# The turned maxima of an attention block: four 32 by 32 block transposes on VectorE in place of a TensorE transpose and a ScalarE copy

## What is computed

```python
h = _layernorm(x) * (1 + ca) + sa
qkv = h @ qkv_w.T                                  # q, k, v of 16 heads
scores = einsum('bhqd,bhkd->bhqk', q, k) * scale
out = einsum('bhqk,bhkd->bhqd', softmax(scores), v)
x = x + ga * (out.reshape(B, S, D) @ proj_w.T + proj_b)
h = _layernorm(x) * (1 + cb) + sb
x = x + gb * ffn(h)        # ffn: a base layer, and the adapter whose encoder loses least
```

## Time and profile before

| what | value |
|---|---|
| median of 3 runs | 971.41 us (971.34 to 973.51) |
| the profiled execution, its own time | 969.45 us |
| its span in the trace | 967.6 us |
| busy: TensorE, VectorE, ScalarE, GpSimd | 933.6, 791.9, 656.6, 373.1 us |

### The profile page before, as it was taken

One profiled execution on the slowest core, in us unless ns is written; L12 is line 12 of the kernel. 1 busy time (PEld: TensorE's weight loads), 2 busy tenths in 40 slices (PEclk: granted clock), 3 DMA queues, 4 the chain that ended last, 5 costly groups with the idle time before them and its releaser, 6 DMA issues.

```text
span 967.6 us, 16714 instructions
## 1 busy us (share of the span) xinstructions
PE 933.6 (96%) x5890; PEld 487.8 (50%) x5890; DVE 791.9 (82%) x1629; ACT 656.6 (68%) x1295; POOL 373.1 (39%) x497
## 2 busy tenths in 40 slices
PE   6899999999999999999999999999999999999998
PEld 5443444444445555555454555555445455644486
DVE  4799989999888888877897987876887778888365
ACT  2148788888688677666779677675777766657930
POOL 4050265226456454121756545121655321115320
PEclk9889999999999999999999999999999999999999
DMA  6933052253454211555150511536133500141001
GB/s 179 144 73 45 23 111 63 57 116 87 77 83 74 58 42 36 73 92 162 46 94 13 94 57 36 83 65 167 46 67 51 78 12 25 46 128 55 30 6 50
DMA packets 51427, 68.78 MB, mean 71 GB/s; under 512 B 12347, under 2 KB 35648, under 8 KB 51332
## 3 DMA queue, kind: packets, MB, share of 16 engines
q1 hardware_dynamic: 50108, 66.84, 32.1%
q0 software_dynamic: 384, 0.79, 0.6%
q10 hardware_dynamic: 852, 0.09, 0.1%
HBM read 29.31 MB, written 12.59 MB: 43 GB/s over the span
## 4 chain that ended last, share of the span: by engine, by line
PE 75%; DVE 11%; ACT 5%; DMA 4%; SPq 3%; issue 2%; POOL 1%; ACTq 0%; DVEq 0%
PE pE L851 25%; PE pM L851 21%; PE pO L851 20%; DVE mx L1350 7%; PE pX L851 7%; DMA QO<-lo 2%; ACT P L1176 2%; SPq L1955 1%; DMA xin<-in_x 1%; DVE junk L1544 1%; ACT h2l_full L1263 1%; SPq L2015 1%; DMA P<-in_wmod 0%; ACT h1l_full L1217 0%; DVE junk L1487 0%
## 5 line engine op out<-in xcount | busy, mean ns | idle before, releaser
L1350 DVE TENSOR_REDUCE mx<-pM 128x1 f32<-128x512 f32 x458 | 298.9, 683 | 41.6 <-PE pM L851 39.4
L1176 ACT ACTIVATE P<-pM 128x512 f32<-128x512 f32 x464 | 260.2, 603 | 71.5 <-PE pM L851 70.1
L1350 DVE TENSOR_REDUCE mx<-pE 128x1 f32<-128x512 f32 x428 | 284.5, 682 | 29.4 <-PE pE L851 28.4
L1176 ACT ACTIVATE P<-pE 128x512 f32<-128x512 f32 x413 | 240.6, 603 | 81.0 <-PE pE L851 79.9
L851 PE MATMUL pO<-P,V 128*17 128x512 f32 x2048 | 260.6, 604 | 0.3 <-ACT P L1176 0.2
L851 PE MATMUL pM<-KO,QO 48*128 48x512 f32 x458 | 181.7, 451 | 7.7 <-DMA QO<-lo 6.0
L851 PE MATMUL pE<-KO,QO 48*128 48x512 f32 x428 | 178.4, 444 | 1.4 <-DVE mx L1350 0.6
L851 PE MATMUL pM<-QO,KO 50*128 50x512 f32 x464 | 173.6, 433 | 0.9 <-DVE mx L1350 0.4
L851 PE MATMUL pE<-QO,KO 50*128 50x512 f32 x413 | 169.8, 438 | 1.3 <-DVE mx L1350 0.7
L851 PEld LDWEIGHTS pM<-QO,KO 50*128 50x128 f32 x464 | 80.2, 187 | 85.3 <-issue 59.6
L851 PEld LDWEIGHTS pE<-QO,KO 50*128 50x128 f32 x413 | 73.5, 186 | 96.9 <-issue 76.4
(11 more groups left out here) (362 smaller groups left out, 1392.5 us busy)
## 6 DMA issues: line engine op xcount, KB each, us to landing
outs<-osb SPq DMA_DIRECT2D x31, 256.0 KB, 2.0
KO<-hi SPq DMA_DIRECT2D x56, 128.0 KB, 4.0
QO<-hi SPq DMA_DIRECT2D x56, 128.0 KB, 5.6
x<-in_x SPq DMA_DIRECT2D x20, 256.0 KB, 3.5
out<-x SPq DMA_DIRECT2D x16, 256.0 KB, 2.1
AT<-outs SPq DMA_DIRECT2D x15, 256.0 KB
asum<-wsum SPq DMA_DIRECT2D x15, 256.0 KB
KO<-lo SPq DMA_DIRECT2D x28, 128.0 KB, 4.0
```

What stands on the lines that cost most here:

```text
L1176: e.activation(P[:, u % 3, j, :], bank(s), ACT.Exp).then_inc(*empties(s))
L1350: e.tensor_reduce(mx[:, hq % 2, k:k + 1, kh], bank(s), AX.X, ALU.max, negate=True).then_inc(*empties(s))
```

## The change

The `mturn` step leaves TensorE and ScalarE. VectorE does it with four transposes of 32 by 32 blocks, from `mhl` in SBUF to `mT` in SBUF, and raises a semaphore of its own, `s_mT`, for which the DMA queues wait. The step no longer takes a PSUM bank, and the planner holds it at the front of the queue "quiet" instead of "short". The lag of 1.2 units, `LEAD` and the other constants stay.

```diff
-BANKED = {"modmm", "modT", "modT2", "ln1turn", "qk", "v", "mturn", "oturn", ...
+BANKED = {"modmm", "modT", "modT2", "ln1turn", "qk", "v", "oturn", ...
-SHORT = {"ln1turn", "mturn", "oturn", "atturn", "xturn", "select", "modT2"}
+SHORT = {"ln1turn", "oturn", "atturn", "xturn", "select", "modT2"}
+QUIET = {"mturn", "oput", ...
...
-                waiting["short"].insert(0, ("mturn", m // 32 - 1))
+                waiting["quiet"].insert(0, ("mturn", m // 32 - 1))
...
# tensor
-                elif kind == "mturn":
-                    pe.wait_ge(s_mhl, s[1] + 1)
-                    e.transpose(o[0:32, 0:128], mhl[:, s[1] % 2, :], ident).then_inc(*fills(s))
...
# scalar
-                    act.wait_ge(*full(*s))
-                    e.activation(mT[0:32, hq % 2, :], bank(s)[0:32, 0:128], ACT.Copy).then_inc(*empties(s))
-                    if hq == 0:
-                        act.wait_ge(*emptied(*s))
+                elif s == ("mturn", 0):
+                    act.wait_ge(s_mT, 1)
...
# vector
+                elif kind == "mturn":
+                    hq = s[1]
+                    if hq >= 2:
+                        for j in range(4):
+                            dve.wait_ge(d_m[hq % 2][j], 16 * (hq // 2))
+                    dve.wait_ge(s_mhl, hq + 1)
+                    for k in range(0, 128, 32):
+                        a = e.transpose(mT[0:32, hq % 2, k:k + 32], mhl[k:k + 32, hq % 2, :])
+                    a.then_inc(s_mT, 1)
...
# sync
-                    sp.wait_ge(*emptied(*s))
+                    sp.wait_ge(s_mT, hq + 1)
```

More of the change, by code:

```diff
@@ L27 @@
           "out": 2}
-BANKED = {"modmm", "modT", "modT2", "ln1turn", "qk", "v", "mturn", "oturn", "atturn", "proj", "xturn", "enc", "gsq",
+BANKED = {"modmm", "modT", "modT2", "ln1turn", "qk", "v", "oturn", "atturn", "proj", "xturn", "enc", "gsq",
           "half", "base", "select", "mid", "out", "setupa", "setupb", "setupq", "setupc"}
-SHORT = {"ln1turn", "mturn", "oturn", "atturn", "xturn", "select", "modT2"}
-QUIET = {"oput", "oget", "orec", "osum", "onorm", "wbload", "gates", "ln1load", "ln1s", "ln1n", "prep", "prepb", "xload", "addx", "bn2", "ln2s", "ln2n", "xsq", "xhi", "xsp", "ehi", "elo", "wsplit", "wload", "sbc", "scale", "pick", "fetch",
+SHORT = {"ln1turn", "oturn", "atturn", "xturn", "select", "modT2"}
+QUIET = {"mturn", "oput", "oget", "orec", "osum", "onorm", "wbload", "gates", "ln1load", "ln1s", "ln1n", "prep", "prepb", "xload", "addx", "bn2", "ln2s", "ln2n", "xsq", "xhi", "xsp", "ehi", "elo", "wsplit", "wload", "sbc", "scale", "pick", "fetch",
          "h1s", "wvload", "wvs", "wqload", "wqs"}
@@ L698, in adaln_block @@
         s_free = [sem(f"free{i}") for i in range(7)]
-        s_pv = sem("pv")
+        s_pv, s_mT = sem("pv"), sem("mT")
         s_sgexp, s_hi, s_qh, s_ql, s_osb, s_xsq = (sem(n) for n in ("sgexp", "hi", "qh", "ql", "osb", "xsq"))
@@ L1183, in scalar @@
                     e.activation(osb[:, :], pO[:, :], ACT.Copy).then_inc(s_osb, 1)
[L1185 to L1189, removed]
-                    act.wait_ge(*full(*s))
-                    e.activation(mT[0:32, hq % 2, :], bank(s)[0:32, 0:128], ACT.Copy).then_inc(*empties(s))
-                    if hq == 0:
-                        act.wait_ge(*emptied(*s))
-                        for j in (2, 3):
-                            e.dma_start(*rows(hq, j)).then_inc(d_m[0][j], 16)
+                elif s == ("mturn", 0):
+                    act.wait_ge(s_mT, 1)
+                    for j in (2, 3):
+                        e.dma_start(*rows(0, j)).then_inc(d_m[0][j], 16)
                 elif kind == "open":
@@ L1347, in vector @@
                     if hq >= 2:
-                        dve.wait_ge(*full("mturn", hq - 2))
+                        dve.wait_ge(s_mT, hq - 1)
                     dve.wait_ge(*full(*s))
```

## The result

| | us |
|---|---|
| before, median of 4 runs beside those of after | 972.46 (971.34 to 973.55) |
| after, median of 4 runs | 1000.51 (999.1 to 1005.35) |
| ratio | 1.0303, 95% interval 1.0284 to 1.0322 |
| span of the profiled execution, before and after | 967.6 and 997.3 |

A forecast was written before the change was run, and what follows sets the result against it. TensorE was taken to set the pace, with VectorE just behind it. 5.6 us lost at tight places less 3.6 us won at loose ones gave +2.1 us (rounded), 973.5 us against the median of 971.41; range 966 to 980.

The forecast's parts named there:

- every quiet step loses a slot at 32 bursts: Planner's list: quiet steps lose slots and banks rotate otherwise, shifting the order slightly; unpriced, 2 us allowed either way.
- on SyncE the order of rows and operand copies hardly changes: SyncE's DMA queue: the quiet slot stands directly behind the same burst's copies and the four issues are the same.
- operand copies landing later, or a list that has shifted long steps: Signs listed as showing the forecast wrong, beside a wait for GpSimd at the turns; no size given.
- the price: VectorE's four transposes at each turn: 0.77 us, three serial starts and one overlapped, 25 us in all.
- The low end, 0.44: VectorE's step if all four transposes overlap: 0.44 us a turn, giving a sum of -1.7 us.
- tight places: 11 groups with VectorE idle under 0.62 us behind the transpose: new work less idle time loses 5.6 us.
- the relief: TensorE without its transpose: 0.21 us won at 17 of 21 loose places, 3.6 us together.
- the sum of +2.1 us: Whole kernel: 5.6 us lost at tight places less 3.6 us won at loose ones (rounded).
- VectorE's gaps are no reserve: Slower rival: VectorE's gaps are waits that come back when delayed, so tight places pay fully; +7.0 us, 978.4, chance 0.25.
- no wait for `mhl`: VectorE at the turns: GpSimd's split maxima are ready in time, so waiting for them costs nothing.
- the copies of ScalarE: 32 copies of 0.27 us leave ScalarE, 8.6 us: costed at nothing, at most 0.5 us gain.
- TensorE's busy time falls by up to 7 us: Expected sign in the profile after: TensorE, without its 32 transposes, is busy up to 7 us less.

The follow-up runs named there:

- vec_old_banks: Changed kernel on the old list, with a 4 by 4 matmul keeping the turn's PSUM bank in the rotation: 979.93 us, ratio 1.0083.
- te_one_late_v: Kernel before with only group 5's turn in "quiet" and the second sample's v steps due 8 units later: 972.89 us, ratio 1.002.
- vec_lag: Changed kernel with a lag of 1.8 units instead of 1.2: 995.12 us, ratio 1.0241.
- vec_late_v: Changed kernel, all turns in "quiet", with the second sample's v steps due 8 units later: 994.32 us, ratio 1.0237.
- te_extra_same: Kernel before plus four unused VectorE transposes at each turn, all reading partitions 0 to 31: 972.26 us, ratio 1.001.
- te_extra_four: Kernel before plus four unused VectorE transposes at each turn, reading the four partition quadrants: 978.02 us, ratio 1.0069.
- vec_old_order: Changed kernel with the turn in "short", so the list of steps is that of the kernel before: 976.33 us, ratio 1.0077.
- both_engines: Kernel before on its list, VectorE turning the maxima only for groups 18 to 31: 968.58 us, ratio 0.9977.
- vec_loose_only: Kernel before on its list, VectorE turning only the 21 groups where the prediction saw room: 971.76 us, ratio 0.999.
- te_new_order: Kernel before, TensorE transpose and ScalarE copy kept, with the turn in "quiet", so on the changed kernel's list: 994.4 us, ratio 1.0228.
- te_late_copies: Kernel before with only the operand copies of head groups 4 and 5 put four and five bursts later: 981.77 us, ratio 1.01.
- te_one_moved: Kernel before with the turn of group 5 alone in "quiet": 986.46 us, ratio 1.0161.

## Why the prediction was wrong

- **Wrong, the step that failed:** "every quiet step loses a slot at 32 bursts and the banks rotate otherwise, so the order of the whole list shifts slightly; I allow 2 us either way", and with it "on SyncE the order of rows and operand copies hardly changes". The list costs 22.2 us, eleven times the allowance. The banks in that sentence cost nothing that can be seen (vec_old_banks); it is the slots. The number of displaced steps is not what counts (te_one_late_v has 8 and costs 1.9 us, vec_lag has 109 and costs as much as vec_late_v with most of the 319) but whether a step that TensorE will wait for is among them. In the one turn with most of the cost these are the operand copies and the `qk` steps in front of them; elsewhere they are the rows of the maxima and GpSimd's `AT` and `h1l`. The prediction had named its own sign of being wrong, "operand copies landing later, or a list that has shifted long steps"; both came. The planner is in the kernel and its list could have been written out for both queues without any chip; the copies at unit 47.0 for 44.0 would have been seen.
- **Right, the price:** 0.77 us a turn, from an overlap that the rows showed only on like partitions and that the working took away for unlike ones; te_extra_same shows that this was the right reason and not luck. The low end, 0.44, would have been right for one quadrant (0.41).
- **Nearly right, tight places:** 5.6 us lost were worked out; the same work added to a kernel that keeps its TensorE transposes loses 6.7 (4.6 to 8.8, te_extra_four), and in its profiled execution 8.6 of 9.4 us are lost by group 17, where the prediction had its tight places.
- **Too high, the relief:** of "3.6 us won at 17 places" vec_old_order shows nothing: +7.5 with the relief against +6.7 without it, with intervals of 3 and 2 us to either side. both_engines shows 2.2 of it, in the second half. So the sum of +2.1 us should have been about +7. The rival "VectorE's gaps are no reserve", +7.0 us, has the number of the kernel on its old list, but got it from a step of 0.88 us that no run has, so its nearness is in part luck. That gaps before group 18 are no reserve fits vec_loose_only; one by one this wasn't tried.
- **Right:** no wait for `mhl`; the copies of ScalarE worth nothing that could be separated. **Wrong:** "TensorE's busy time falls by up to 7 us"; it rose by 8.9, beside more matmuls at the lower clock (22 in 5 us where 36 were done at the higher).
- Without the move to "quiet" the time, 976.3, would have lain inside the range, but 3 us over the forecast of 973.5.

**Settled:** the split into list and work, the one turn with most of the list's cost, the waits by which it costs. **Argued only:** that the waits for GpSimd's `AT` and `h1l` make the rest of the list's cost; they stand at the steps of the lag, also in te_new_order (1.89 us at 261.72, 2.58 at 393.19), but no run takes them away alone. **Open:** which displaced steps make GpSimd late, the 4 us behind group 26, and why the clock falls before group 4 in some kernels and not in others.

## What to carry to other kernels

In a kernel with a planned order, a step that changes its queue is two changes: write out the list before and after, look first at the loads, the copies and the other engines' steps that the bound engine waits for, and price how much slack each has left in the trace (here, with each kernel's own lag at group 6 taken off, a copy issued at 199.0 was early enough but for 0.54 us, and one at 203.1 or 203.4 was not). An experiment that moves steps wants the same check of its own list: te_late_copies moved nine copies three units too far. Then separate the two on the chip: new work on the old list, old work on the new list; their sum closed to 0.2 us here, within intervals of some us. If the step goes to an engine that stands just behind the pace setter, do it only where that engine has room: behind group 17 it gained 2 us, at all groups it lost 7.

## What the runs showed of the hardware

- A wait of TensorE can cost more than its length. At the wait of 4.65 us before group 7 the changed kernel fell 8.8 us behind; at one of 4.59, te_one_moved fell 6.4; at one of 9.70, te_late_copies 11.2. The granted clock is at 0.50 for some 9 us of matmuls behind the first and the last (212 to 222 us, and 262.6 to 271). Over the span it is 0.976 after and 0.987 before in the profiled executions, 0.966 to 0.976 in the four runs of after and 0.975 to 0.988 in those of before beside the experiments.
- It need not. The wait of 4.00 us at 799.01 (2.09 before) was followed by 0.50 too (800 to 805), and yet the lag was 25.0 us at group 26 and 25.4 at group 28.
- That the clock falls is not certain: at 134 us nearly the same list with the same wait of 1.27 us kept 1.00 in one execution and fell to 0.50 in another.
- Four 32 by 32 transposes of f32 start 0.21 us apart from four quadrants and about 0.10 apart from one (0.47 for all four, with a record of 0.156 by the median).
- The matmul that waited for the last operand copy, of 128 KB, started 7.3 us after the copy's issue in te_late_copies (255.23 to 262.57) and 7.1 after it in the changed kernel (205.07 to 212.19). Beside each a transfer of 256 KB was under way. The median landing of `QO<-lo` over the changed kernel is 6.2 us.
